# Sixteen head pairs of attention written out as a straight program in a one-core transformer block

## What is computed

```python
q = _rmsnorm(x @ wq_a.T, q_a_ln_w) @ wq_b.T
...
ckv_kpe = x @ wkv_a.T
ckv, k_pe = (ckv_kpe[..., :KVR], ckv_kpe[..., KVR:])
kv = _rmsnorm(ckv, kv_a_ln_w) @ wkv_b.T
...
scores = jnp.einsum('bqhd,bkhd->bhqk', q_full, k_full) * softmax_scale
causal = jnp.tril(jnp.ones((S, S), dtype=bool))
scores = jnp.where(causal[None, None], scores, jnp.finfo(scores.dtype).min)
attn = jax.nn.softmax(scores, axis=-1)
out = jnp.einsum('bhqk,bkhd->bqhd', attn, v).reshape(B, S, H * VD)
return out @ wo.T
```

## Time and profile before

| | us |
|---|---|
| median of 3 runs | 2024.18 |
| lowest, highest | 2022.32, 2027.04 |
| the profiled execution | 2021.53 |
| its span, first to last instruction | 2019.5 |
| in it: before the loop, up to | 433 |
| the loop on PE, 14 trips | 433 to 1330 |
| after the loop | 1330 to 2019.5 |

### The profile page before, as it was taken

The page is one execution under the profiler, slowest core; times in us unless marked ns, Lnnn a source line. Parts: engine busy times, 40 slices in busy tenths (PEclk is TensorE's granted clock), DMA queues, the critical chain, the costliest instruction groups (busy, mean ns, idle before and its releaser), DMA issues. The chain is left out here.

```text
span 2019.5 us, 44379 instructions
## 1 busy us (share of the span) xinstructions
PE 1839.7 (91%) x15472; PEld 1438.7 (71%) x15472; DVE 1221.3 (60%) x2653; ACT 992.3 (49%) x2135; POOL 870.3 (43%) x641
## 2 busy tenths in 40 slices
PE   6999878699999999999999999998499999978999
PEld 4678677576777767676676766776388888867887
DVE  5555266487878878787887888878431111115543
ACT  2211055487877877787877878777321001003110
POOL 2221110366768677676867768675000000004311
PEclk9999989899999999999999999999799999989999
DMA  6442142302112121211212121221552322324421
GB/s 230 169 149 94 72 133 78 89 21 79 61 68 65 48 80 48 80 46 66 71 57 77 35 80 65 64 65 54 171 190 88 113 90 83 104 95 145 141 88 63
DMA packets 111695, 182.45 MB, mean 90 GB/s; under 512 B 27472, under 2 KB 64464, under 8 KB 109584
## 3 DMA queue, kind: packets, MB, share of 16 engines
q1 hardware_dynamic: 111632, 181.61, 27.6%
HBM read 122.06 MB, written 59.51 MB: 90 GB/s over the span
## 5 line engine op out<-in xcount | busy, mean ns | idle before, releaser
L940 PE MATMUL psS<-keyT,q 128*128 128x512 f32 (+2 forms) x2304 | 483.7, 356 | 59.7 <-POOL q L1145 48.3
L940 PEld LDWEIGHTS psS<-keyT,q 128*128 128x128 f32 x2304 | 390.7, 194 | 156.2 <-DVE negmax L1071 46.9
L1021 ACT ACTIVATE prob<-prob,negmax 128x640 f32<-128x640 f32 (+7 forms) x512 | 392.0, 767 | 152.8 <-DVE negmax L1071 150.4
L1081 DVE STREAM_TRANSPOSE pT<-prob 128x640 f32<-128x640 f32 (+7 forms) x512 | 375.8, 758 | 51.5 <-PE psV L957 47.1
L1071 DVE CUSTOM_DVE_ANT_0 prob<-psS,mask 128x640 f32<-128x640 f32 (+7 forms) x512 | 370.9, 741 | 45.7 <-PE psS L940 35.0
L413 PE MATMUL f_psy<-f_weff,f_xT 128*128 128x512 f32 x1344 | 313.8, 393 | 0.0
L1136 POOL TENSOR_TENSOR pT<-pT,cosT 64x512 f32<-64x512 f32 x128 | 164.7, 1286 | 331.6 <-ACT pT L1006 318.9
L1307 PE MATMUL o_psy<-o_w,o_o 128*128 128x512 f32 x1344 | 304.8, 389 | 0.0
L1307 PEld LDWEIGHTS o_psy<-o_w,o_o 128*128 128x128 f32 x1344 | 252.3, 188 | 52.4
L413 PEld LDWEIGHTS f_psy<-f_weff,f_xT 128*128 128x128 f32 x1344 | 250.9, 188 | 53.9 <-issue 1.7
L957 PE MATMUL psV<-pT,val 32*64 32x512 f32 (+3 forms) x8192 | 265.7, 408 | 6.2 <-DVE pT L1081 6.2
(11 more groups left out here) (99 smaller groups left out, 1875.1 us busy)
## 6 DMA issues: line engine op xcount, KB each, us to landing
wo<-in_wo SPq DMA_DIRECT2D x16, 1024.0 KB, 5.7
pT<-row_scales SPq DMA_DIRECT2D x128, 128.0 KB, 2.8
oT<-pT SPq DMA_DIRECT2D x64, 256.0 KB, 2.4
o_in<-oT SPq DMA_DIRECT2D x32, 512.0 KB, 5.2
f_xt<-in_x SPq DMA_DIRECT2D x16, 512.0 KB, 4.2
f_w_in<-in_w SPq DMA_DIRECT2D x16, 512.0 KB, 6.1
w_sum<-f_w_in SPq DMA_DIRECT2D x16, 512.0 KB, 5.1
x<-f_xo SPq DMA_DIRECT2D x16, 512.0 KB, 2.7
```

Of the source, the lines that this page charges most:

```text
L940: ins = nc.tensor.matmul(psS[:, slot, start + x0:start + x1], q[:, e, a, t * P:(t + 1) * P], k.keyT[:, m, b * S + x0:b * S + x1], start=(i ...
L1021: nc.scalar.activation(row, row, ACT.Exp, bias=negmax[:, n % 8:n % 8 + 1], scale=-1.0, accum_out=rowsum[:, column(n, s):column(n, s) + 1]) ...
L1081: nc.vector.transpose(pT[:, n % 2, t, 0:width], prob[:, n % RING, 0:width]).then_inc(turned, 1)
```

## The change

The hardware loop becomes a loop of the program's author: the body is written 14 times, each with its pair's number as a constant. No table, tile, wait or operation of an engine changes, and neither does their order. The registers, the arithmetic on them and the branch go; the program is longer.

```diff
@@ -753,7 +753,7 @@
 
 def rounds(eng, body):
     body(Round(0, first=True))
-    with eng.Fori(1, PAIRS - 1) as it:
+    for it in range(1, PAIRS - 1):
         body(Round(it))
     body(Round(PAIRS - 1, last=True))
```

## The result

| | before | after |
|---|---|---|
| median over runs on the same chip | 2024.18 us, 9 runs | 2038.92 us, 9 runs |
| lowest, highest | 2020.76, 2029.44 | 2030.69, 2049.17 |
| the profiled execution | 2021.53 | 2038.92 |
| its span | 2019.5 | 2037.1 |

The straight kernel takes 1.0075 times the time of the loop (95% interval 1.0057 to 1.0093), 14.7 us more. The forecast was 2014, with 2030 as its upper end.

A forecast was written before the change was run, and what follows sets the result against it. TensorE (PE) sets the pace, busy 94% of the loop; only its idle time and low clock can be won. Minus 7 (edge and F), 0 (K), plus 1 (V blocks), minus 4 (clock): 10 us off, 2014; range 1996 to 2030.

The forecast's parts named there:

- edge and F: PE's waits at the trip's end, S8 behind V and then F: 7.7 us can go, 7 us counted as gain.
- V blocks: PE's 28 blocks of 256 matmuls with weight loads: instruction fetch adds 0 to 0.25 us each, 1 us in all.
- the clock: PE's low-clock stretches behind F's wait: some go once F is at its floor, 4 us gained, ends 0 and 7.
- the floor: F's wait in straight code, until ACT's copy and DVE's join: 0.52 us; F can't start before 1.65 us behind V.
- the margin: Path to F: 1.4 us shorter, R0 needed up to 0.8 us sooner, so the floor is reached with 0.6 to spare.
- K: S8's wait in the step with K, behind X0's stores and L842: 0 us, ends minus 6 and plus 10.
- rival C: Instruction packets delay X0's stores behind L842, the low clock spreads: 17 us slower, 2041; chance 0.13, in part or full.
- trip 1: The loop's first pass, which fetches everything: its V block took 8.46 us against 8.21 in round 0.

The follow-up runs named there:

- All straight with the order moved: All five engines straight, and SP's order with K and L right behind X1, against the kernel before: 1958.57 us, 0.9695; again 1957.76 us, 0.9704.
- X0 first: The changed kernel, all engines straight, with X0 put ahead of K and L in SP's order: 2020.92 us, 0.9980 of the kernel before.
- the kernel with 256 bytes: The kernel before, all loops kept, plus two plain 256-byte transfers a step issued by ACT into an unread scratch tensor: 2041.87 us, 1.0139.

## Why the prediction was wrong, step by step

Three terms make up the miss from -10 to +21.3 in the stretch: edge and F (8.5 us), the V blocks (6.2) and the clock (13.7), with Q's wait (2.4) and 0.5 of smaller ones behind them.

- **Edge and F (-7, measured +1.5): the reading of the floor was right; the step that failed is the margin on the path to it.** S8 follows V directly in 10 trips of 14, sets of L861 span 1.34 us in most, POOL's gap is gone, and 8 of 14 F waits stand at 0.48 to 0.69. The other six are 1.1 to 2.24. Of the 1.4 us that the path was to get shorter, the 1.2 on SP didn't come (10.46 against 9.97, above). The prediction took it that stores issued sooner land sooner by as much. But their landings are later by more: the set behind L lands 2.50 us behind its last store (1.60 before, means), X1's 2.02 (1.38). Most of that comes without PE's packets: with SP alone straight it is 2.21 and 1.96.
- **K (0): right within 1 us.** SP issued sooner, the landing came later: from L842's issue to L865's 6.85 us on average, 6.27 before, in place of the 7.13 that the earlier trace rows had once; a large packet does lie in that window, as the prediction guessed. The two cancel, as rival C said in kind, not in size.
- **V blocks (+1, measured +7.2): the mechanism was named, the size failed.** I took trip 1 for the test of fetching and one block of it, 0.25 us over, for the upper end. 12 of the 28 blocks were longer than 8.21, up to 9.61. Nine of the twelve are in the step with K, where the block starts about when L842's 1 MB is issued, and hold 4.9 of the excess. The sizing that was there to be made: two packets of the earlier trace rows in each V block, one every 4.1 us, on engines that just then carry 1 MB.
- **The clock (-4, measured +9.7): wrong in sign.** Low stretches lie in the first half of four trips, and in these F waited 2.2, 1.1, 1.3 and 2.2 us; no trip with F's wait below 1 us has one there. Low time rose in second halves too, from 20.5 to 41.0 us. From the kernels with 0, 37.5, 68.3, 88.7 and 133.1 us of low clock, PE's other work is 595.6, 613.5, 623.2, 633.0 and 649.9: 0.40 to 0.48 us lost for each us. I counted on the clock as a gain that follows the waits; it follows them both ways.
- **Not in the sum: Q's wait**, 2.4 us in five trips. Q0 waits for DVE's joins, which stand behind X1's landing. In three of the five X1's four issues spanned 2.0 to 2.7 us, where 1.05 is usual; why SP was slow there stays open.
- **Rival C** had the right sign (2041 against 2038.9), but by other terms: it put 10 us on K and 1 on V; its 10 for the clock is near the 9.7. Its mechanism, a packet on an engine that a store waits for, is compatible with the windows of PE alone straight and not shown by adding packets.

Left open: how much of the 9.7 us of clock is due to V stalls and how much to the waits. All straight with the order moved, V blocks with up to 0.95 us of excess brought no low clock, which speaks for the waits; with X0 first, stalls of over 3 us did bring it. In the changed kernel no block had more than 1.4 us of excess. Why two short issues a step on ACT cost 1.2 to 1.4% wasn't followed to its end.

## What to carry to other kernels

Before unrolling an engine's loop, count its instructions in the densest stretch and ask what else the DMA engines carry then; a body that stays with the engine costs nearly nothing (0.3 us an edge here), one that doesn't is paid where instructions are short and where a small store is waited for. Unroll the engine whose register work lies on the path (here SP: -0.7%) and keep the loop of the one that issues thousands of instructions. And look first at what is queued ahead of the transfer that is waited for: moving two loads in one table gave nearly four times what any unrolling gave.

## What the runs showed of the hardware

- A PE loop body of some 1440 instructions stayed with the engine; one of some 2900 fetched every trip and stood still for 4.3 to 4.8 us behind each branch back.
- Instruction packets of 16 KB hold about 252 of PE's matmuls and weight loads (20161 by 80), some 65 bytes each. PE's go by q8. Of the other engines, the stretch with the four straight shows 47 packets of 8 KB on q14 and no more on q8 than before.
- An engine that has run dry goes on 1.3 to 1.7 us after its packet has ended (23 stalls of PE inside V blocks, in five kernels). 20 of the stalls are under 0.7 us; two were 3.3 and 3.5, and the clock fell with these.
- Small stores that are issued closer together land later behind the last one: X1's four, in 1.10 us from first to last issue, 1.96 us behind (SP alone straight); in 1.40 us, 1.38 behind (before).
- Waits that were longer by 0.3 us on the mean of a half trip went with nearly twice the time at the lower clock (37.5 to 71.7 us, the kernel with 256 bytes); with S8's and F's waits down to 4.9 and 3.8 us there was none in 847 us.
